# A four-layer hybrid transformer block on one Trainium2 core: the value products in longer runs, POOL's late steps moved, the start and the last feed-forward jobs rearranged

## The reference, cut to what matters

```python
x = X                                              # (4, 2048, 256)
x = x + attn_a(layernorm(x), q_proj, k_proj, v_proj, o_proj)
x = x + ffn(layernorm(x), W_r, W_k, W_v, mu_r, mu_k)
x = x + attn_b(layernorm(x), W_k, W_v, W_c, leaky_key_beta, key_scale, v_coef, val_scale)
x = x + ffn(layernorm(x), W_r, W_k, W_v, mu_r, mu_k)

def attn_a(x):        # 16 heads of 16, causal
    q, k, v = heads(x @ q_proj.T), heads(x @ k_proj.T), heads(x @ v_proj.T)
    return merge(softmax(causal(q @ k.T / 4)) @ v) @ o_proj.T

def attn_b(x):        # keys decayed over time and normed; also the queries
    k = normed(decay(heads(x @ W_k.T), beta)) * exp(10 * key_scale)
    v = normed((1 - v_coef) * shift_left(v0) + v_coef * v0) * exp(10 * val_scale)   # v0 = heads(x @ W_v.T)
    y = softmax(causal(k[1:] @ k.T)) @ v          # row t takes the result of row t - 1
    return merge(shift_right(y)) @ W_c.T

def ffn(x):
    xr, xk = mix(x, shift_right(x), mu_r), mix(x, shift_right(x), mu_k)
    return sigmoid(xr @ W_r.T) * (relu(xk @ W_k.T) ** 2 @ W_v.T)
```

## Time and profile before

| | |
|---|---|
| median of 3 runs | 3587.72 us (3585.63 to 3592.41) |
| the profiled execution | 3594.36 us, its span 3592.6 us |
| PE | 3191.8 us busy (89%), 19172 instructions |
| ACT | 2287.9 us (64%), of it 2135.9 in the 2176 exponentials of 1023 ns |
| DVE | 1445.8 us (40%) |
| POOL | 828.4 us (23%) |
| PE, line 988 (scores) | 1205.2 us in 5120 matmuls |
| PE, line 1030 (value products) | 1177.8 us in 10240 matmul records |
| mean granted PE clock | 0.931 of full speed |

### The profile page before, as it was taken

The page is one execution under the profiler, slowest core; times in us unless marked ns, Lnnn a source line. Parts: engine busy times, 40 slices in busy tenths (PEclk is TensorE's granted clock), DMA queues, the critical chain, the costliest instruction groups (busy, mean ns, idle before and its releaser), DMA issues.

```text
span 3592.6 us, 51970 instructions
## 1 busy us (share of the span) xinstructions
PE 3191.8 (89%) x19172; PEld 1224.7 (34%) x19172; DVE 1445.8 (40%) x3578; ACT 2287.9 (64%) x2479; POOL 828.4 (23%) x1278
## 2 busy tenths in 40 slices
PE   5899998888998789997999999889988879899786
PEld 3322233333333233332333333333333323333234
DVE  4322234454444543334233333545354444322424
ACT  1588776666766366774666766667666655677460
POOL 3211122322222122221222222222222312212111
PEclk8999999999999799997999999999999988999797
DMA  4222212222121122222212222221122220222111
GB/s 110 85 68 70 70 53 65 63 62 68 48 59 52 51 57 64 73 68 57 81 58 64 77 80 72 62 64 49 52 61 65 63 54 29 62 60 62 42 39 47
DMA packets 230832, 223.18 MB, mean 62 GB/s; under 512 B 34373, under 2 KB 214085, under 8 KB 230472
## 3 DMA queue, kind: packets, MB, share of 16 engines
q1 hardware_dynamic: 230472, 218.41, 21.2%
HBM read 146.80 MB, written 71.32 MB: 61 GB/s over the span
## 4 chain that ended last, share of the span: by engine, by line
PE 69%; DVE 17%; issue 7%; ACT 4%; POOL 1%; SPq 1%; DMA 1%; DVEq 0%; ACTq 0%; POOLq 0%
PE ps L1030 23%; PE ps L988 22%; PE ps L852 12%; PE ps L843 10%; ACT probs L789 3%; DVE pmax L1321 2%; PE ps L837 2%; DVE ln_st L1094 1%; DVE xn L1103 1%; DVE k_blk L1300 1%; DVE rest L1124 1%; DVE nw_u L1084 1%; DVE nw_y L1088 1%; DVE nw_u L1086 1%; DVE o_blk L1369 1%
## 5 line engine op out<-in xcount | busy, mean ns | idle before, releaser
L789 ACT ACTIVATE probs<-ps 128x1024 f32<-128x1024 f32 x2176 | 2135.9, 1023 | 837.6 <-PE ps L988 622.8
L988 PE MATMUL ps<-q_st,k_st 99*128 99x512 bf16 (+3 forms) x5120 | 1205.2, 353 | 112.5 <-issue 95.8
L1030 PE MATMUL ps<-probs,v_st 128*17 128x512 f32 (+3 forms) x10240 | 1177.8, 541 | 130.1 <-POOL probs L700 101.9
L988 PEld LDWEIGHTS ps<-q_st,k_st 99*128 99x128 bf16 x5120 | 423.8, 98 | 1073.5 <-ACT probs L789 483.1
L700 POOL TENSOR_SCALAR_AFFINE_SELECT probs<-probs 128x256 f32<-128x256 f32 (+1 forms) x896 | 400.7, 464 | 1674.6 <-ACT probs L789 1662.8
L1030 PEld LDWEIGHTS ps<-probs,v_st 128*17 128x17 f32 x10240 | 185.1, 96 | 624.5 <-issue 346.9
L1369 DVE STREAM_TRANSPOSE o_blk<-ps 128x512 f32<-128x512 f32 x128 | 90.9, 710 | 501.7 <-PE ps L1030 501.7
L843 PE MATMUL ps<-xT,wT 128*128 128x512 f32 x512 | 255.8, 625 | 7.9 <-DVE rest L1121 5.5
L1214 DVE TENSOR_TENSOR x_buf<-x_buf,ps 128x512 f32<-128x512 f32 x64 | 43.5, 680 | 429.3 <-PE ps L852 429.3
L624 POOL TENSOR_TENSOR parts<-rest,parts 128x512 bf16<-128x512 f32 x96 | 119.8, 1248 | 374.3 <-DVE parts L1126 374.3
L852 PE MATMUL ps<-wT,o_in 128*128 128x256 f32 x512 | 162.4, 473 | 1.8 <-DVE o_blk L1369 0.9
(11 more groups left out here) (138 smaller groups left out, 2243.1 us busy)
## 6 DMA issues: line engine op xcount, KB each, us to landing
part_a<-parts SPq DMA_DIRECT2D x192, 128.0 KB
x_buf<-in_L_attn_a_X SPq DMA_DIRECT2D x32, 512.0 KB, 4.4
q_st<-part_a SPq DMA_DIRECT2D x128, 128.0 KB
o_chan<-o_out SPq DMA_DIRECT2D x64, 256.0 KB, 2.4
o_in<-o_chan SPq DMA_DIRECT2D x64, 256.0 KB, 4.5
q_st<-part_b SPq DMA_DIRECT2D x128, 128.0 KB
k_st<-part_a SPq DMA_DIRECT2D x64, 192.0 KB, 2.9
part_b<-parts SPq DMA_DIRECT2D x96, 128.0 KB
```

The source lines that it names most:

```text
L789: nc.scalar.activation(probs[:, g % NP_BUF, :], ps[:, bk:bk + 2, :].rearrange("p a n -> p (a n)"), ACT.Exp, scale=SCALE[ATT[g // (NHG * NG ...
L988: last = pe.matmul(o[:, col:col + w], k_st[0:KROWS, j, kb * P:(kb + 1) * P], q_st[0:KROWS, j, qc * CH + q0:qc * CH + q0 + w], start=True, ...
L1030: last = pe.matmul(ps[32 * j:32 * j + VW, bank, q0:q0 + w], v_st[:, k % 2, kb, hg * HG + j, :], p, start=(kb == 0), stop=(kb >= TB * qc), ...
```

## The change

1. **Product sets in longer runs.** The product sets of full key blocks are done in pairs, so every fourth slot in place of every second; the four product sets of a diagonal are done together after the last of its five groups, where one stood after the second, two after the fourth and one after the fifth. An instance has 16 slots with products instead of 36 of 68. `NP_BUF` goes from 6 to 7, and `seg_at` changes banks for the parts at the first product of a chunk (`FIRST_PV`).
2. **POOL's late steps.** The values' factors move from 59 to slot 64 of the job, the low parts from 60 and 61 to 67 and 69, and their stores from 63 to 71 and 73; the loads of keys that wait for them move from slot 65 to 75.
3. **The last FFN jobs.** The last `MB` job of batch element 2 starts 33 slots earlier, and the four `MB` jobs of batch element 3 start 16, 37, 58 and 82 slots from the start of the last instance (of 68 slots), instead of 2, 23, 44 and 65 slots behind its end: three of them within it.
4. **The start.** The first three weights are loaded on ACT's queue; SP's queue starts with x, and `W_o`, `W_c` come after the small parameters; the third and fourth chunk of x are loaded in slot order. POOL signals twice, first as soon as `ident` is set. The other seven weights are transposed and copied in the slot of the second job. Four banks (4 to 7) take parts ahead of slot 0, in turn, and ACT copies the transposed x of these jobs in place of DVE.
5. **Flagged instances.** An unflagged head no longer writes zeros nor places them by DMA; it only counts its semaphores up.

```diff
+        full = [i for i, st in enumerate(sets) if st[1] == qc and st[2] < d]
+        for i in full[0::2]:
+            sets[i] = (sets[i + 1][0], *sets[i][1:])
+        for i, st in enumerate(sets):
+            if st[1] == qc and st[2] >= d:
+                sets[i] = (g, *st[1:])
...
-NP_BUF = 6
+NP_BUF = 7
...
-       "len": 56, "split": 58, "low": 59, "store": 63}
+       "len": 56, "split": 58, "vb": 64, "low": 67, "store": 71}
...
-    jobs += [Job("MB", 2, c, 7, start(7, c) - 3) for c in range(NCH)]
-    jobs += [Job("MB", 3, c, 8, NTOT + 2 + 21 * c) for c in range(NCH)]
+    jobs += [Job("MB", 2, c, 7, start(7, c) - 3 if c < 3 else start(7, 2) + 32) for c in range(NCH)]
+    jobs += [Job("MB", 3, c, 7, start(7, 3) + (16, 37, 58, 82)[c]) for c in range(NCH)]
...
-    if slot < 1:
+    if slot < FIRST_PV[0]:
...
-    done = [qc for qc in range(NCH) if i > FIRST_OF[qc]]
+    done = [qc for qc in range(NCH) if i >= FIRST_PV[qc]]
...
+SIDE_BANKS = (4, 5, 6, 7)
...
-        if slot < 0 or slot >= NTOT:
+        if slot < 0:
+            bank = SIDE_BANKS[n % len(SIDE_BANKS)]
...
-                if j.b > 0:
+                if j.b or j.c >= 2:
...
-                yield j.t0 + T_B["store"]
                 for m in range(KT):
+                    yield j.t0 + T_B["store"] + 2 * m
...
-                    there = FIRST_SLOT if hg else j.t0 + (T_P["u3"] + T_P["store"] if j.kind == "P" else T_B["store"]) + 2
+                    there = FIRST_SLOT if hg else j.t0 + (T_P["u3"] + T_P["store"] if j.kind == "P" else T_B["store"] + 2) + 2
...
-            for i in (WQ, WK, WV):
-                load_weight(i)
             for c in range(2):
                 load_x(JOB["P", 0, c])
-            for i in (WO, FR, FK, FV, BK, BV, BC):
+            for i in (FR, FK, FV, BK, BV):
                 load_weight(i)
             sp.dma_start(mu[:, 0, :], t["mu_r"].rearrange("(k p) -> p k", p=P),
...
+            load_weight(WO)
+            load_weight(BC)
             sp.wait_ge(s_rows_set, 1)
             sp.dma_start(rows_d, q_st[0:3, 0, :]).then_inc(s_rows, 16)
-            for c in range(2, NCH):
-                load_x(JOB["P", 0, c])
...
-            step(pool.memset(k_st[MROW:KROWS, :, :], 1.0))
-            settle()
...
-                yield j.t0 + T_B["low"]
+                yield j.t0 + T_B["vb"]
...
-                    yield j.t0 + T_B["low"] + 1 + m
+                    yield j.t0 + T_B["low"] + 2 * m
...
-            def weight(i, bank):
-                act.wait_ge(s_wt_ps, i + 1)
-                nc.scalar.copy(wT[:, i].rearrange("p k n -> p (k n)"), ps[:, bank, :]).then_inc(s_wt, 1)
-
-            for i in range(6):
-                weight(i, i)
+            def weight(n, i):
+                act.wait_ge(s_wt_ps, n + 1)
+                nc.scalar.copy(wT[:, i].rearrange("p k n -> p (k n)"), ps[:, n % 4, :]).then_inc(s_wt, 1)
+
+            for i in W_FIRST:
+                nc.scalar.dma_start(w_nat[:, i], t["weights"][i].rearrange("(m p) d -> p m d", p=P)).then_inc(s_w[i], 16)
+            for n, i in enumerate(W_FIRST):
+                weight(n, i)
...
-                for i in range(6, 10):
-                    weight(i, i - 6)
+                yield JOBS[1].t0
+                for n, i in enumerate(W_LATER):
+                    weight(len(W_FIRST) + n, i)
                 act.wait_ge(s_par, 6 * 16)
...
+                if j.b == 0:
+                    for kt in range(KT):
+                        yield j.t0 + T_P[f"t{kt}"]
+                        part = j.at[f"t{kt}"]
+                        act.wait_ge(s_part, part.n + 1)
+                        nc.scalar.copy(xT[:, j.at["chan"] % 2, kt, :], ps[:, part.bank, :]).then_inc(s_side[part.bank], 1)
```

More of the change, by code:

```diff
@@ L86 @@
 DIAG = [i for i, g in enumerate(GROUPS) if g[0][0][1] >= TB * g[0][0][0]]
+FIRST_PV = [min(at for at, c, *_ in SETS if c == qc) for qc in range(NCH)]
 KEY_LAST = [max(i for i, g in enumerate(GROUPS) if any(u[1] // TB == c for bk in g for u in bk)) for c in range(NCH)]
@@ L516, in place_maxima @@
                     for j in range(HG):
-                        sp.wait_ge(s_mx["row"], n * HG + j + 1)
-                        for r in range(3):
-                            sp.dma_start(q_st[MROW + r:MROW + r + 1, j, :].rearrange("o (t q) -> o t q", t=NT),
-                                         m_part[r][:, :]).then_inc(s_mx["placed"], 16)
+                        flag = sp.value_load(flags_of(k)[:, hg * HG + j:hg * HG + j + 1])
+                        with sp.If(flag > 0):
+                            sp.wait_ge(s_mx["row"], n * HG + j + 1)
+                            for r in range(3):
+                                sp.dma_start(q_st[MROW + r:MROW + r + 1, j, :].rearrange("o (t q) -> o t q", t=NT),
+                                             m_part[r][:, :]).then_inc(s_mx["placed"], 16)
+                        with sp.Else():
+                            sp.sem_inc(s_mx["placed"], 48)
                 with sp.Else():
@@ L1158, in p_job @@
                 layernorm(j)
-                for kt in range(KT):
-                    yield j.t0 + T_P[f"t{kt}"]
-                    copy_out(j.at[f"t{kt}"], xT[:, j.at["chan"] % 2, kt, :])
+                if j.b > 0:
+                    for kt in range(KT):
+                        yield j.t0 + T_P[f"t{kt}"]
+                        copy_out(j.at[f"t{kt}"], xT[:, j.at["chan"] % 2, kt, :])
                 for i in range(4):
```

44 lines of the change are left out of this document (25 added, 19 removed).

## The result

The changed kernel takes 3498.42 us (median of 4 runs, 3493.83 to 3507.8) against 3590.06 (4 runs, 3585.63 to 3594.28): a ratio of 0.9746, 95% interval 0.9726 to 0.9765, so 92 us less. The forecast was 3426, which is 162 to 164 less; the time lies in the stated range of 3310 to 3540, but the gain is 56% of what was forecast.

What follows compares the result with a forecast made beforehand. PE bounds the kernel (busy 3191.8 of 3592.6 us). Terms -131, -154, -15, +13, +135, +53, -33, -64, +34 sum to -162: 3432 from 3594.4, 3426 against the median; range 3310 to 3540, its own 3370 to 3480.

Steps and rivals of the forecast that it cites:

- POOL's late steps: In MA jobs, moving POOL's factors and low parts later removes PE's 16 mask waits (100) and regains clock (31): -131 us.
- Product runs: PE's joined product sets save 0.24 us each, 640 in all (-154); 152 fewer parts stand behind a run (-15).
- Score waits: Four score groups in a row make PE wait 0.49 us for ACT to free banks, mostly in part-free stretches: +135 us.
- The sign that I had set: A total wait of PE for ACT far from 135 us would make the prediction wrong.
- Side banks: Banks held longer leave PE's parts waiting for copies behind short scores: +53 us, bounds nothing to about twice that.
- the rival in which it comes back: DVE's rest is later, so POOL and PE wait again at the diagonal's masks: +131, about 3555 us; chance 0.13.
- Borders: At 28 inner borders of instances, scores alone instead of a product run cover PE's branch: +13 us.
- Start and end: Earlier first scores save 33 us, a shorter tail 64; the jobs moved into PE's full order cost +34.
- The flagged heads' edit: Four instances save a few small writes and DMAs for three heads each: nothing, at most -15 us.
- the first falls: Rival: ACT keeps up in the runs of four score groups, so the +135 go, about 3290 us; chance 0.14.
- (the third): Rival: jobs moved inside find no room and SP's pace holds at the start: 3470 to 3520 us; chance 0.08.
- The clock doesn't fall in the stretches without parts: Against the rival that PE's 0.49 us waits bring 1.2 GHz there, some 750 us if always; chance 0.07.

## Why the prediction was right and wrong

**Product runs (-154, -15).** The 0.24 us for a joined run is right: a pair with no wait takes 3.67 us, as worked out, once the exponential is short. Of the 162 other pieces with parts some 120 are 0.2 to 0.5 us shorter, 30.8 net in all 162. The sum of the two terms can't be measured by itself, since each joined run also brings its waits.

**Score waits (+135).** The mechanism was right and the size a little high: the loop is 1.72 us and not 1.79, so a pair without parts costs 0.19 more than before and not 0.25, and a diagonal 0.3 and not 0.5. With the 0.24 for each joined run put back, the 210 pieces of the table paid 102 us for the waits (77 and 25), where 123 were forecast for 217; the 12 that the term had for pieces with parts can't be told from the next term. The sign that I had set, a total near 135, is met only by this count: the profile's own idle time for ACT ahead of the scores is 67.0.

**Side banks (+53).** This is the step that failed most. Each piece against what its joined run alone would save (0.34 for a pair, 0.48 for a diagonal): t 26 x 1.35 = 35, u 24 x 1.0 = 24, v 12 x 0.82 = 10, bk 16 x 1.08 = 17, and the 162 others, which gained 31 of some 60, make 29: some 115 in all, with the 12 of the score waits in it, the "about twice that" of the bound. It exceeds its term by 50 to 62, and the score waits fell short of theirs by about 20, so the two errors partly cancel, which is luck: with the score waits as forecast the time would be some 20 us higher. The list of gaps held only waits of a part for the bank of the part before. It lacked the other side, the products that wait for a part's copy, which stands behind DVE's chain on the output. That alone is 31 us by the run with the chain moved. The cause is the later change of bank, which came with the longer runs: the first transpose now lies in the bank of the next chunk's products. The wait itself was there to be seen before, in the 16.2 us in 12 places above: there the copy of a `P` job's second transpose lies in the next chunk's bank. At 233.72 us the products start 0.1 us behind DVE's copy (line 1109), and the profile says ACT. The parts u, v and bk have no experiment of their own; that their 51 us are waits of the banks is argued from the table and not shown.

**POOL's late steps (-131).** The wait goes, and the rival in which it comes back didn't happen (1.7 us left). The term was mis-sized: alone the edit gives 104. The waits give 89 of the 100 forecast, since 15 short ones stay (13.3 us in all), and that leaves 15 for the clock, where 31 were forecast. The 2 us of clock for each border did not come back in full: the branch keeps PE idle for 2.58 us by itself, and the clock falls behind it; the `MA` stage has 0.96, not the 0.98 that I took from the other stage. And the ledger gave the whole of it to this edit: beside the joined diagonal it is worth 22 us, most of it by SP's stores and loads and not by POOL. For the sum this doesn't matter, since only one of the two was counted; for the parts it does. The joined diagonal comes three slots later, behind the branch, and I had priced that edit only for what it does to PE. (The prediction's count of masks is off by one: by the order above five, not four, of the last diagonal's later mask instructions stand ahead of the first low part.)

**Borders.** POOL, branch and joined runs were to give -131 + 13 - 14 = -132; it is -110.

**Start and end.** -33 and -64 forecast, -29 and -58 measured; the work moved inside was put at +34, and the last two instances grew by 41. But 7 of these are the longer runs' (207.7 against 200.5 in the kernel with them alone), and without them the work costs 34 (234.1), as forecast. Within it PE waits 3.92 us once, in the last instance; the profile names no releaser, but the products start 0.1 us behind DVE's reading of an FFN part (line 1275), which stood behind a layer norm. The first scores start at 96.0 us, forecast 92. The flagged heads' edit shows nothing clear, as forecast: PE's waits for the placed maxima are 16.7 us before and 17.1 after. The net of the end and the work inside, -30, is -25 by the run that undoes it.

**The sum.** -162 against -87 between the two profiled executions: 37 of the 75 missing lie in the pieces between the borders (+33 by the terms, +70 measured), 22 in the borders, 7 in the last two instances (the longer runs again), 9 in start and end.

**The rivals.** The score waits do cost (the first falls), POOL's wait is gone (the second), and start and end gave nearly what was forecast (the third). The clock doesn't fall in the stretches without parts: 1.00 in both windows, with a wait of 0.25 us in every 4.1, and in all 210 pieces without parts, 914 us, it is at the lower level for 0.8 us. The rule of the Trainium skill, "TensorE: Matmul & The Clock Gate", section "A second HAM failure mode: psum-queue depth-cycling", which would have made these stretches slow, is not borne out here.

## What to carry to other kernels

Joining short runs on PE saves a small fixed cost each time (0.24 us here), but it also moves what hangs on the run, here the point at which the banks change sides, and uses up the lead in buffers; with three pairs of score banks, four groups in a row were already one too many. Before a run is joined, go through each piece of the program with its neighbours and ask which bank or buffer is needed later or earlier by it, in both directions: who waits for the copy, and what stands ahead of the copy on its engine. When two edits can remove the same wait, price each with the other in place: here 104 us and 22 us are the price of the same edit. And look at what else the edit moves: most of the 22 came from stores and loads in a queue, and not from the engine that it was made for.

## What the runs showed of the hardware

PE's clock held at 1.00 through stretches with a wait of 0.25 us in every 4.1 us, but it was at the lower level (granted 0.50 from 559.5 to 563.2) behind an idle time of 2.58 us at a branch: two scores took 1.01 us instead of 0.60, and a projection part 3.62 instead of 1.96. A product matmul of 512 columns has a mean of 599 ns in the changed kernel and of 598 in the one without the longer runs: the saving lies between the runs. And the pieces away from the borders repeat from kernel to kernel within about half a us in several hundred (700.2, 700.2 and 700.1 for the pairs without parts in three kernels), while the borders, where the clock falls, spread: in the changed kernel and four others with the same program at the borders (the ones with later transposes, with DVE's chain later, with the shorter exponential and with the last jobs put back) they came to 517.0, 505.4, 514.5, 508.2 and 507.3, 12 us apart. So a difference of ten us between two of these kernels says little unless the pieces away from the borders show it.
